# A gated cross-attention and stream-mixing layer: x1's statistics by squares and row sums, with GpSimd's coefficients and low parts, the values and the output projection at other steps

## What is computed

```python
# patches: windows of 128 columns; W* are 256x512 (Wo 512x256); 8 heads of 32 rows
qp, vp = patches(layernorm(x)), patches(ctx)
q, k, val = Wq @ qp + bq, Wk @ qp + bk, Wv @ vp + bv
attn = softmax(where(mask, qh^T kh / sqrt(32), -1e9))
x1 = x + tanh(g_xattn) * ((Wo @ gelu(attn vh) + bo) * mask)
# feed-forward: each row of 2048 is n=4 streams of C=512
z = layernorm(x1); zn = z * rsqrt(mean(z*z) + 1.2e-7)
H_res = sinkhorn(zn @ W_res.T + base, 50 iterations, tau 0.1)   # 4x4 for each row
H_pre, H_post = softmax(zn @ W_pre.T + ..), softmax(zn @ W_post.T + ..)
mixed = ((1-g) I + g H_res) @ z_streams + H_post * (sum(z_streams * H_pre) @ W_branch)
out = x1 + tanh(g_ffn) * mixed
```

## Time and profile before

| | before |
|---|---|
| median of 3 runs | 1876.54 us (1875.27 to 1878.99) |
| the profiled execution, its own time | 1877.37 us |
| its span in the profile | 1875.6 us |
| busy share PE, DVE, ACT, POOL | 75%, 75%, 56%, 40% |
| mean granted PE clock | 0.884 |

### The profile page before, as it was taken

One profiled execution on the slowest core, in us unless ns is written; L12 is line 12 of the kernel. 1 busy time (PEld: TensorE's weight loads), 2 busy tenths in 40 slices (PEclk: granted clock), 3 DMA queues, 4 the chain that ended last, 5 costly groups with the idle time before them and its releaser, 6 DMA issues.

```text
span 1875.6 us, 35269 instructions
## 1 busy us (share of the span) xinstructions
PE 1407.9 (75%) x12323; PEld 859.3 (46%) x12448; DVE 1410.1 (75%) x3678; ACT 1056.0 (56%) x2017; POOL 757.3 (40%) x1237
## 2 busy tenths in 40 slices
PE   2779999888988888888888788888888886521223
PEld 0546656555645454455555454445555553320111
DVE  3334555666788897888888888888778887779997
ACT  3557776666766666665666666655666664311111
POOL 3224334555454544455454535454454524320000
PEclk9889999999989998999999898989989997656656
DMA  8457765566656666666656566665665443411123
GB/s 258 137 153 193 218 179 161 160 182 186 179 155 184 188 177 187 188 189 182 185 157 181 164 185 174 176 188 164 170 174 168 120 125 90 124 66 69 56 84 118
DMA packets 173920, 299.85 MB, mean 160 GB/s; under 512 B 23568, under 2 KB 74640, under 8 KB 169648
## 3 DMA queue, kind: packets, MB, share of 16 engines
q1 hardware_dynamic: 156336, 264.03, 45.3%
q0 software_dynamic: 17408, 33.56, 10.2%
HBM read 179.81 MB, written 67.11 MB: 132 GB/s over the span
## 4 chain that ended last, share of the span: by engine, by line
PE 43%; DVE 24%; ACT 10%; POOL 9%; issue 9%; DMA 2%; SPq 2%; DVEq 0%; ACTq 0%; POOLq 0%
PE pr L611 10%; PE pr L625 7%; PE pr L638 6%; PE f L740 4%; DVE ssum L1166 4%; PE av_ps L725 4%; POOL kp L536 4%; DVE otile_odd L1213 3%; POOL ctx_hl L476 3%; DVE negm L1035 2%; PE av_ps L729 2%; DVE sa L1167 2%; PE s_ps L698 2%; DVE otile_even L1213 2%; SPq L404 2%
## 5 line engine op out<-in xcount | busy, mean ns | idle before, releaser
L1166 DVE TENSOR_REDUCE ssum<-kp 128x16 f32<-128x64 f32 x768 | 181.9, 237 | 183.2 <-POOL kp L536 178.1
L476 POOL TENSOR_TENSOR ctx_hl<-ctx_raw,ctx_hl 128x512 bf16<-128x512 f32 x128 | 149.6, 1174 | 219.8 <-ACT ctx_hl L793 219.8
L611 PE MATMUL pr<-x_hl,wq 128*128 128x512 bf16 x708 | 193.0, 425 | 43.9 <-POOL x_hl L471 36.0
L536 POOL TENSOR_TENSOR kp<-ke,sa 128x64 f32<-128x64 f32 x343 | 136.6, 398 | 220.0 <-DVE sa L1167 220.0
L1035 DVE TENSOR_REDUCE negm<-s_ps 128x4 bf16<-128x512 f32 x256 | 166.9, 652 | 73.6 <-PE s_ps L698 72.1
L536 POOL TENSOR_TENSOR kp<-ke,sv 128x64 f32<-128x64 f32 x329 | 145.3, 442 | 187.7 <-DVE sv L1167 187.0
L698 PE MATMUL s_ps<-k_st,q_st 97*128 97x128 bf16 x1024 | 104.3, 226 | 152.8 <-DVE negm L1035 138.6
L611 PE MATMUL pr<-x_hl,wk 128*128 128x512 bf16 x736 | 186.0, 406 | 13.1 <-DVE logit L1101 8.0
L638 PE MATMUL pr<-o_sb,wo 128*128 128x512 bf16 x735 | 185.6, 389 | 11.5 <-POOL o_sb L482 6.9
L838 ACT ACTIVATE probs<-st_ps,key_bias 128x512 f32<-128x512 f32 x256 | 173.5, 678 | 30.5 <-PE st_ps L712 30.2
L471 POOL TENSOR_TENSOR x_hl<-xc,x_hl 128x512 bf16<-128x512 f32 x128 | 148.6, 1161 | 92.3 <-ACT x_hl L806 92.3
(11 more groups left out here) (142 smaller groups left out, 3047.1 us busy)
## 6 DMA issues: line engine op xcount, KB each, us to landing
xs<-in_dram SPq DMA_DIRECT2D x128, 256.0 KB, 4.6
xc<-in_dram SPq DMA_DIRECT2D x32, 1024.0 KB, 10.6
ctx_raw<-in_dram SPq DMA_DIRECT2D x32, 1024.0 KB, 6.8
x1c<-in_dram POOLq DMA_DIRECT2D x64, 512.0 KB, 9.3
x_dram<-x1c SPq DMA_DIRECT2D x32, 1024.0 KB, 4.9
q_st<-q_hl SPq DMA_DIRECT2D x384, 64.0 KB
k_st<-k_hl SPq DMA_DIRECT2D x384, 64.0 KB
x1t_even<-x_dram SPq DMA_DIRECT2D x16, 1024.0 KB, 5.8
```

The source lines that it names most:

```text
L476: ins = nc.gpsimd.tensor_tensor(ctx_hl[:, 1, t, :], ctx_raw[:, t, :], ctx_hl[:, 0, t, :], ALU.subtract)
L536: nc.gpsimd.tensor_tensor(kp[:], ke[:], v, ALU.mult).then_inc(kp_made, 1)
L611: ins = nc.tensor.matmul(bank(what)[:], w[:, a, t, i * P:(i + 1) * P], x_hl[:, G % 2, m, t, :], start=(t == 0 and a + m == 0), stop=(t == ...
L1166: cf.link(nc.vector.tensor_reduce(s_t, k, AX.X, ALU.add))
```

## The change

x1's mean and variance are no longer taken by `bn_stats`. `read_wo` writes a row sum beside its output (`accum_out`). ACT squares each of the four 128x512 parts of `x1c`, shifted by x's mean, with a row sum of its own (`square_x1`). POOL adds the sums up and forms the variance (`stat_b`, part 0: nine small instructions where two were). The coefficients after Sinkhorn are made by POOL, one step after the last half iteration. Low parts, values, output projection, `add_x`, the logits and everything of the feed-forward behind them get other steps, and ACT does the high parts, `first_products` and `first_out` ahead of the bank reads.

```diff
-HI_X_AT, LOW_X_AT = [1, 4, 5, 6], [2, 5, 6, 7]
-HI_CTX_AT, LOW_CTX_AT = [0, 0, 1, 1], [0, 1, 1, 4]
-T_AT, LOGITS_AT, SELECT_AT = [3, 3, 4, 4], 7, 8
-STAT_B_AT = [1, 3]
+HI_X_AT, LOW_X_AT = [1, 4, 5, 6], [3, 5, 6, 7]
+HI_CTX_AT, LOW_CTX_AT = [0, 0, 1, 1], [1, 2, 2, 3]
+T_AT, LOGITS_AT, SELECT_AT = [3, 3, 4, 4], 5, 9
+SQUARES_AT = [3, 3, 4, 4]
...
+COEF_AT = SINK_AT + len(SINK)
-BESIDE = dict(load=-8, first=-6, xpre=-5, pre=-4, branch_0=0, branch_1=1, out_0=-1, out_1=0,
+BESIDE = dict(load=-8, first=-6, xpre=-5, pre=-3, branch_0=0, branch_1=1, out_0=-1, out_1=0,
-TILE_AT = {(f, t): UNITS * (f + 1) + 53 + UPC * t for f in range(LAST_BESIDE + 1) for t in range(DT)}
+TILE_AT = {(f, t): UNITS * (f + 1) + 54 + UPC * t for f in range(LAST_BESIDE + 1) for t in range(DT)}
...
-                 6: [("v", G + 1, 0)], 7: [("v", G + 1, 1)]}.get(r, [])
-    if 0 <= G - 1 < NG and r in (4, 5):
-        made += [("o", G - 1, 2 * (r - 4)), ("o", G - 1, 2 * (r - 4) + 1)]
+                 4: [("v", G + 1, 0)], 7: [("v", G + 1, 1)]}.get(r, [])
+    if 0 <= G - 1 < NG and r in (5, 6):
+        made += [("o", G - 1, 2 * (r - 5)), ("o", G - 1, 2 * (r - 5) + 1)]
...
-                if r == 1 and 0 <= G - 2 < NG:
+                if r == 2 and 0 <= G - 2 < NG:
                     store_x1(G - 2)
...
+            def coefficients(f):
+                pool.wait_ge(scale_made, HALVES * (f + 1))
+                flat = kp[:].rearrange("p t i j -> p t (i j)")
+                cp.link(nc.gpsimd.tensor_tensor(kp[:], kp[:], bcast(sv[:], 2, N), ALU.mult))
...
+                nc.gpsimd.tensor_tensor(cmat[:, f % 2].rearrange("p t i j -> p t (i j)"), flat,
+                                        bcast(eye_sb[:], 1, DT), ALU.add).then_inc(coef_ready, 1)
...
                 scale_at(f, its, 1)
+                for H, t in at_step(g, -1, LOW_CTX_AT):
+                    split_ctx(H, t)
+                if 0 <= G - 1 < NG and r == 4:
+                    low_gelu(G - 1, 0)
+                scale_at(f, its, 2)
+                if 0 <= G - 1 < NG and r == 4:
+                    low_gelu(G - 1, 1)
                 for H, t in at_step(g, -2, LOW_X_AT):
                     split_x(H, t)
...
                 scale_at(f, its, 3)
-                if 0 <= G - 1 < NG and r in (6, 7):
-                    add_x(G - 1, r - 6)
+                if 0 <= G - 1 < NG and r == 7:
+                    add_x(G - 1, 0)
+                if 0 <= G - 2 < NG and r == 0:
+                    add_x(G - 2, 1)
...
+            def square_x1(H, t):
+                f, w = divmod(H, NC)
+                n = DT * H + t
+                act.wait_ge(x1_added[t // 2], 16 * (H + 1))
+                if n >= 2:
+                    act.wait_ge(sq_done, n - 1)
+                nc.scalar.activation(squares[:, t % 2], x1c[:, t, :], ACT.Square, bias=nmean[:, f % 3, t:t + 1],
+                                     accum_out=sums[:, f % 2, 1, t, w:w + 1]).then_inc(sq_done, 1)
...
+                    dve.wait_ge(sq_done, DT * G)
                 nc.vector.scalar_tensor_tensor(out=x1c[:, t, :], in0=bank(what)[:],
...
+                                               accum_out=sums[:, G // NC % 2, 0, t, G % NC:G % NC + 1]
+                                               ).then_inc(wo_read, 1)
...
+                if f:
+                    dve.wait_ge(coef_ready, 2 * f)
                 nc.vector.tensor_reduce(m8, lpp, AX.X, ALU.max)
...
-                for H, h in at_step(g, 2, STAT_B_AT):
-                    stat_b(H, h)
```

117 lines of the change are left out of this document (54 added, 63 removed).

## The result

The changed kernel takes 1857.5 us (median of 4 runs, 1850.53 to 1862.02), the kernel before 1875.9 us (4 runs on the same chip, 1874.94 to 1878.99). The ratio is 0.9896, 95% interval 0.9871 to 0.9921: faster by 1.0%, 18 us, where 94 were forecast. The profiled execution has a span of 1856.3 us.

What follows compares the result with a forecast made beforehand. Full chunks were taken as bound by waits round four engines, DVE busiest, and after the change by a loop on ACT. From 1877.4 us, 22 chunks x 4.25 and 1.5 for the tail gave 1782.4, as median 1782; range 1735 to 1868.

Steps and rivals of the forecast that it cites:

- the wait at r1: DVE's wait at r1 for a scaling behind the q projection: 3.0 of 4.33 us saved per full chunk.
- DVE's work: DVE's busy time in a fully loaded chunk: from 43.2 to 40.1 us.
- the tail: After the last maximum: one more Sinkhorn step, less statistics and coefficients on DVE, plus new waits; net -1.5 us.
- the loop on ACT: Round trip from r1's normalisation through x's load: a full chunk takes 46.5 us, above DVE's own 44.65.
- the rule weighed: Two-input DVE streams and GpSimd subtractions exclude each other: three more meetings a chunk would make 1817 us.
- bn_stats and coefficients: Leaving DVE: 3.5 us less work per full chunk, counted in full where DVE sets the pace.
- Row sums in the read: Four row sums a chunk in `read_wo` on DVE: 0.4 us added, between nothing and 1.0.
- Squares: Four squares with row sums on ACT, in r3 and r4: 2.9 to 3.7 us a chunk.
- Light stages: Batches 0 and 1 and half of batch 2, bound by PE: 0 us, with 2 either way.
- the 4 us of 293: Sign in the changed profile: the tail, from the last maximum on, stays within 4 us of 293.
- The clock above 0.93: Sign in the changed profile: PE's granted clock in the full stage above 0.93.
- half: Rival: in full chunks the new loop or collisions take back half; 48.6 us a chunk, 1828 us, chance 0.23.

Runs made afterwards that it cites:

- e1: Kernel before plus only ctx's parts: high parts ahead of the bank reads, low parts at r1, r2, r2, r3; 1811.5 us.
- e9: e1 plus ScalarE's new order and the routing coefficients on GpSimd; tables, tiles and statistics as before; 1805.3 us.
- e3: Changed kernel with x1's statistics back on VectorE (bn_stats and bn_aggr, no squares, no row sums in the projection's read); 1849.3 us.
- e8: e1 plus x1's statistics by ScalarE's squares and row sums in the projection's read, tables as in e1; 1824.1 us.
- e4: Changed kernel with each square over 1 column of 512, so x1's variance is wrong; 1822.8 us.
- e6: e1 plus ScalarE's new order (normalisation, first products and first outputs ahead of bank reads and inverses); 1805.5 us.
- e2: Changed kernel with ScalarE's order undone, except for ctx's high parts; 1850.9 us.
- e10: e9 with the output tiles and the selection, and so the Sinkhorn steps, one step later; 1849.3 us.
- e5: e1 plus the routing coefficients on GpSimd, nothing else; 1807.5 us.
- e15: Changed kernel with GpSimd's statistics of x1 behind the last scaling, two steps apart, inverse roots one step behind each; 1861.5 us.
- e7: e1 plus all of the change's tables; ScalarE's order, statistics and coefficients as before; 1899.2 us.

## Why the prediction was wrong in size

The forecast saved 95 us on the profiled execution (94 on the medians): 66 for the wait at r1, 68 for DVE's work and 1.5 for the tail, less 41 for the loop on ACT. Measured apart: 64 for r1 (e1), 6 for ScalarE's order and the coefficients together (e9), 44 lost by the moved tables (e3 over e9), 8 lost by the statistics (the changed kernel over e3).

- **The wait at r1, -3.0 us in 22 chunks.** Right in mechanism: r1 fell by 3.0 us in the mean. The total, 64 us measured alone and 66 forecast, is partly luck: a full chunk gave 2.5, and what was missing came from batch 2 and the light batches. GpSimd's wait for ctx's high parts fell from 219.8 us over the run to 82.4 in e1 and 54.0 in the changed kernel.
- **The step that failed most: the moved tables had no term.** The prediction priced what was removed and added, and took what was moved (v's first half, the output projection, x's low parts and their place, gelu's low parts, the tiles' step) as free but for the chain at r1 and the loop on ACT. Together they cost 44 us (e9 to e3), of it 5 for the tail's step. Their mechanism stood in the text as the rule weighed (SBUF — State Buffer, "Who interferes with whom", in the Trainium skill): by it three streams a chunk would be held 0.54 us each, 1817 us. It was not taken into the sum. The traces bear the rule out: between e9 and e3 the streams grow by 30.9 us with no change in their work, and the cut subtractions remove it. The Trainium skill, in the same section, frees a DVE instruction with one SBUF input only outside the two-port performance modes, a condition that the prediction left out. The row sums here, with one such input, keep their 237 ns throughout. What the sum needed was a table by step: which streams stand at which r, which subtractions beside them, before and after.
- **The second step that failed: bn_stats and coefficients, -3.5 us a chunk.** The size in busy time was right (DVE lost 73.7 us over the run, against the 100 forecast, with 24.6 us of longer streams in between). The step that fails is that they "count in full where DVE sets the pace": DVE doesn't set it alone. With the loop on ACT the forecast had 27 us for this work in the full chunks; the statistics' move cost 8 to 13 us (e3, e8), since the squares lie on ACT where DVE then waits. The coefficients alone gave 4 us at most, where 0.6 us a chunk would make 13.
- **Row sums in the read, +0.4.** Right: four reads of 83 ns, 0.33 us.
- **Squares, 2.9 to 3.7 us a chunk on ACT.** Right: 4 x (0.716 + 0.195) = 3.64. Their price wasn't: they were put into a loop through x's load that sets a floor of 46.5 us a chunk. That loop isn't the bound (the time of 875.64 that it rests on is also GpSimd's scaling, not DVE's): the loads of `xc` land after 5.6 us in the median in place of 10.6, and ACT waits for them almost only in batches 0 and 1. The squares cost by being in front of what DVE waits for, 35 us for 55 us of length (e4).
- **Light stages, 0 ± 2.** Wrong for batch 0 and ahead of it: +8.3 and +3.3 us. ScalarE's order has a part in it, 4 us of batch 0 by e1 and e6, 10 by e2, with some 5 us between executions of the same order.
- **The tail, -1.5.** +4.0 measured, still within the 4 us of 293 that were named as a sign. The extra step was right: 5.3 us (298.3 in e10 against 293.0 in e9). The 8.6 us of work that left DVE there weren't gained: the statistics gave 2.3 (298.9 in e3, 296.6 in the changed kernel), the coefficients nothing (292.4 in e1 and in e5).
- **The clock above 0.93.** 0.92 as before. r1 got it back (0.68 to 1.00), r3 lost it (0.79 to 0.52; its first row on PE starts after a wait of 2.77 us for the maximum).

The rival called "half", the new loop or collisions, is the case that the time fell in, nearer to no change than its own 1828. Its loop isn't what happened; collisions are, with the statistics' waits beside them. Not shown is how the tables' 44 us divide between streams that are held and scalings that queue behind subtractions. Open is also how the 8 us of the statistics in the changed kernel divide between ACT's squares and GpSimd's sums; e15 says only that moving the sums gives nothing.

## What to carry to other kernels

A step that is moved has a price even if nothing in it changes: where two engines exclude each other for whole instructions, write down which of their instructions stand beside each other before and after, and price every new pair both ways (the held instruction, and the small one queued behind the holder). Work taken from the busiest engine gains only if the engine that receives it isn't what the busiest one then waits for; here, at an engine that was 61% busy, two thirds of what the squares were shortened by came out of the time. Take a change of many parts apart and time each: one table row here, with its places in two queues, was worth 64 us, and the rest of the change gave 46 of them back. And where two kernels turn out equal once a suspected cost is removed from both, look for a bound that they share before calling the cost proven.

## What the runs showed of the hardware

- A DVE product of two SBUF tensors took 4.67 us, 21 times its own length, beside four GpSimd subtractions in a row (e7, 684.39): it didn't get in between two of them. In six such places it took 4.5 to 5.4 us.
- It goes the other way as well: a GpSimd scaling took 0.75 us in place of 0.29 beside DVE's streams (832.11 in the changed kernel, 838.23 before).
- An ACTIVATE with a row sum is two instructions, the second 195 ns; on DVE the second took 83 ns.
- In the changed kernel GpSimd's 128x64 coefficient instructions took 0.29 to 0.77 us in the mean, where the first and the last of them on DVE took 0.22. How much of that is GpSimd's own length and how much waiting beside DVE isn't told apart.
